# Flamingo block on one core: independent products between a group's last evacuation and its first dependent product, early octets loaded by ScalarE, finer waits

## The chip, the cores and the metric

One NeuronCore of a Trainium2 chip. The metric is the device time of one execution in microseconds, as the median of several runs. Engines in this text: TensorE (PE; PEld are its weight loads), VectorE (DVE), ScalarE (ACT), GpSimd (POOL), SyncE (SP; SPq and ACTq mark DMAs that SyncE and ScalarE issue). Sixteen DMA engines move the data.

## What is computed

A gated cross-attention block followed by a gated feed-forward block, 16 batches of 128 tokens of width 1024, all in float32. Cut to what matters:

```python
def attn(q, k, v):                       # 16 heads, dk = 16, 4 parts m per head
    qh, kh, vh = proj(q, Wq, bq), proj(k, Wk, bk), proj(v, Wv, bv)
    qh, kh, vh = (x + 0.1 * amp * einsum('bhsdi,hij->bhsdj', x, interference) for x in (qh, kh, vh))
    scores  = einsum('bhqdm,bhkdm->bhqkm', qh, kh) / sqrt(dk)
    weights = softmax(scores, axis=3)
    return einsum('bhqkm,bhkdm->bhqdm', weights, vh) @ Wo.T + bo

def ffn(x):
    base   = einsum('bsi,oi->bso', x, W_org)
    q      = einsum('bi,ki->bk', x.mean(axis=1), Wq)
    coeffs = softmax(einsum('bk,ek->be', q, lora_keys) / sqrt(K))
    h      = einsum('bsi,eir->bser', x, lora_down)
    return base + einsum('be,bser,ero->bso', coeffs, h, lora_up)

x = x + tanh(g_xattn) * attn(layernorm(x), ctx, ctx)
x = x + tanh(g_ffn)   * ffn(layernorm(x))
```

## The kernel before

Products of float32 precision are made from three float32r products: each operand is split into `hi` (ScalarE rounds, L149) and `lo` (VectorE subtracts, L152), and TensorE runs hi x hi, hi x lo, lo x hi (`three_products`, L159 to L161; 24 matmuls of 512 columns for a contraction over 1024).

The program has three phases with different schemes.

*Projections (0 to 614 us).* The order is a list of jobs (`Line`). A job is TensorE work into one of eight PSUM banks in turn, an optional ScalarE evacuation and a VectorE evacuation. Every engine goes through the list in order. TensorE waits for the bank (the job eight before must be emptied) and for `reads`, the number of the last job whose result it needs; since jobs are emptied in order, waiting for a number waits for everything before it. Steps for SyncE (loads and stores) stand in a `plan`, sorted by job number, and run in that order on its queue; each can wait. The batches are taken in four groups of four. A context tile is loaded and split into `place_a` or `place_b` (`ctx_jobs`). `k_job(g, c)` makes 128 output columns (chunk c) of the keys of group g, `q_job` the same of the queries, `v_job(b, half)` half of the values of batch b; keys and queries leave by `stage_hi` and `stage_lo` (L514, L512), two buffers in turn, each stored by six DMAs (L523). `mixed_chunk` multiplies a raw weight chunk by the head mixing matrix (L292) and splits the result. It is done for Wk and Wv in the first group, for Wq beside the values of the last group, where the inputs x are also normalised (`x_norm`, VectorE with a square root on ScalarE) and transposed (`x_jobs`, L326). During the last eight query products `wo_chunk` splits the output weights, DMAs from `v_out` lay rows of zeros and ones into the scratch tensors (L681, L682), four query tiles are cleared (L689, L695), and the first four octets are loaded (`load_early`, by SyncE, three DMAs each, L192 to L195).

*Attention (614 to about 1050 us).* 128 octets (8 heads of one batch) pass through an order written out by hand in slots: first pass of scores (L868), a maximum (L1008, L875, L1020), the maxima put into the query tile by a small DMA from `neg` (L803), second pass (L888), exponentials (L966), values (L903, each four octets), output projection (L851 to L853). Octet loads go by SyncE three slots ahead, once the octet six before has had its second pass.

*Feed-forward (to the end).* Job lists again. The LoRA products of the first group are begun before their coefficients are known: `h_job(0, 0, ..., "products")`, the scores (`first_scores`), `h_job(0, 1, ..., "products")`, then a VectorE-only job for the coefficients (`first_coefs`), two chunks of weights to split, and `spread_job`, which lays the coefficients along the rows (L1287 on TensorE, `coefc` by VectorE, L1290). The next product takes the bank that `spread_job` has eight jobs before it.

Of the kernel before, what the change touches and what calls it, by code (L numbers as in the profile page):

```python
# [15 lines left out]
class Job:  # L16

    def __init__(self, pe, dve, act=None, reads=0, pe_wait=None, act_wait=None, dve_wait=None,
                 act_pre=None, dve_pre=None, passed=None):
        self.pe, self.dve, self.act, self.reads = pe, dve, act, reads  # L20
        self.pe_wait, self.act_wait, self.dve_wait = pe_wait, act_wait, dve_wait
        self.act_pre, self.dve_pre, self.passed = act_pre, dve_pre, passed

class Line:
# [43 lines left out]
    def run_vector(self, dve):  # L68
        scaled = 0
        for n, job in enumerate(self.jobs):  # L70
            if job.dve_pre:
                job.dve_pre(dve)
            if job.act:
                scaled += 1
                dve.wait_ge(self.scaled, scaled)
            elif job.dve:
                self.wait_filled(dve, n + 1)
            if job.dve_wait:
                job.dve_wait(dve)
            if job.dve:  # L80
                job.dve(self.bank(n)).then_inc(self.emptied, 1)
            else:
                job.passed(dve).then_inc(self.emptied, 1)

def build(nc, x, ctx_cols, g_xattn, g_ffn, wq, wk, wv, biases, interference, amp, wo_rows, bo,
          w_org_rows, down_rows, lora_up, keys_cols, w_key, out):
    NB, S, D = x.shape
# [29 lines left out]
    with top:  # L117
# [303 lines left out]
        with proj, ExitStack() as st:  # L421
# [117 lines left out]
            def q_job(g, c):  # L539
                return projection_job(wq_end, t_end[NB + g * GB + GB - 1], 0, *x_place(g), bias_mixed[:, 1, c:c + 1],  # L540
                                      q_rows, c, g, 1)

            def v_job(b, half):
# [24 lines left out]
                job = Job(pe_fn, empty, reads=max(t_end[b], wv_end), dve_wait=stage_free)  # L568
# [34 lines left out]
            wk_end = {}  # L603
# [13 lines left out]
            for c in range(KC):  # L617
                job = k_job(0, c)
                if c == 0:

                    job.dve_pre = lambda dve: [link(dve.memset(v[:], 1.0)) for v in v_out]
                if c + 4 < KC:
                    wk_chunk(c + 4)
                wv_end = mixed_chunk(line, ring, wv, c, wv_hi, wv_lo)
            for g in range(NG):
                for b in range(g * GB, (g + 1) * GB):
                    v_job(b, 0)
# [6 lines left out]
                    for c in (2 * xb, 2 * xb + 1):  # L634
                        wq_end = mixed_chunk(line, ring, wq, c, w0_hi, w0_lo, reads=mix_scaled)
                    v_job(b, 1)
                    x_norm(xb, line.jobs[-4])
                    x_jobs(xb)
                if g + 1 < NG:
                    for c in range(KC):  # L640
                        job = k_job(g + 1, c)
                        if g + 2 == NG and c == 0:
                            def scale_mix(dve):

                                line.wait_filled(dve, wv_end)
                                link(dve.tensor_scalar(mix[:], mix[:], DK ** -0.5, None, ALU.mult))
# [6 lines left out]
            for g in range(NG):  # L653
                for c in range(KC):
# [42 lines left out]
                    if g == NG - 1 and KC - 1 - EARLY <= c < KC - 1:  # L697

                        def load_early(sp, o=c - (KC - 1 - EARLY)):
                            sp.wait_ge(s_cleared, EARLY)  # L700
                            sp.wait_ge(s_stage[o % 2], 96 * ((NG * KC + o) // 2 + 1))
                            load_kq(sp, o, (first_k, second_k, early_k[2], early_k[3])[o],
                                    early_q[o] if o else first_q, s_kq[o])
                        plan.append((len(line.jobs) + 0.7, load_early))
# [409 lines left out]
        with attend, ExitStack() as st:  # L1114
# [90 lines left out]
            def first_coefs():  # L1205
# [5 lines left out]
                return line.add(Job(None, coef_dve, dve_wait=lambda dve: dve.wait_ge(s_smalle, 1)))  # L1211
# [268 lines left out]
```

## Time and profile before

| | us |
|---|---|
| median of 3 runs | 1466.41 |
| lowest, highest | 1462.62, 1468.31 |
| profiled execution, its device time | 1468.58 |
| its span, first to last instruction | 1465.4 |
| TensorE busy in it | 1399.3 |
| VectorE, ScalarE, GpSimd busy | 674.2, 396.7, 234.8 |

All rows below come from the one profiled execution. A span leaves out some 3 us ahead of the first and behind the last instruction. TensorE's ends are modelled, and matmuls overlap: of 24 in a product each shows 0.39 us and starts some 0.23 us after the one before. A wait is given with the instruction that came last before it ended.

### The profile page before, as it was taken

The numbers are of one execution on the slowest core, as the hardware profiler recorded it, in microseconds if no ns is written. First come the engines' busy times: TensorE is split into PE (matmuls) and PEld (weight loads), VectorE is DVE, ScalarE is ACT, GpSimd is POOL, SyncE is SP. The second block draws the span as 40 slices with busy tenths as digits, with TensorE's granted clock in tenths as the row PEclk, the third lists the DMA queues.
The fourth block names the chain that finished last, engine by engine and source line by source line (L and its number), as shares of the span: only waits on it lengthen the run. The fifth ranks groups of instructions, "written<-read, shape, count | busy, mean of one in ns | idle before, by whom it ended". The sixth has DMA issues, their size and how long they took to land.

```text
span 1465.4 us, 22266 instructions
## 1 busy us (share of the span) xinstructions
PE 1399.3 (95%) x8592; PEld 1150.2 (78%) x8592; DVE 674.2 (46%) x1379; ACT 396.7 (27%) x736; POOL 234.8 (16%) x400
## 2 busy tenths in 40 slices
PE   7999999999999999878999999999979999999998
PEld 7887887878888888666777777877767878878787
DVE  5322131221555544456766666776766334244110
ACT  3311111111222222234545555454443110021100
POOL 0000000000000000014655555555600000000000
PEclk9999999999999999969999999999989999999999
DMA  6763645536547677966776776766542212202101
GB/s 201 205 170 130 142 145 137 151 124 143 178 152 186 161 188 183 259 198 201 216 229 193 232 222 205 222 200 199 179 179 87 86 44 75 83 17 85 43 30 57
DMA packets 181719, 224.86 MB, mean 153 GB/s; under 512 B 24048, under 2 KB 122352, under 8 KB 181616
## 3 DMA queue, kind: packets, MB, share of 16 engines
q1 hardware_dynamic: 166160, 189.11, 44.1%
q10 hardware_dynamic: 15456, 34.35, 7.3%
q8 instruction: 68, 1.11, 0.3%
q14 instruction: 35, 0.29, 0.1%
HBM read 136.89 MB, written 85.46 MB: 152 GB/s over the span
## 4 chain that ended last, share of the span: by engine, by line
PE 82%; DMA 8%; DVE 3%; SPq 3%; issue 2%; ACT 1%; POOL 0%; POOLq 0%; ACTq 0%; DVEq 0%
PE bank L159 19%; PE bank L161 19%; PE bank L160 19%; PE bank L903 4%; PE bank L868 4%; PE bank L888 3%; PE bank L292 3%; DMA q_in<-q_rows 3%; DMA early_q<-q_rows 3%; PE bank L851 2%; PE bank L853 2%; PE bank L852 2%; DMA first_q<-q_rows 2%; PE bank L326 2%; PE bank L875 1%
## 5 line engine op out<-in xcount | busy, mean ns | idle before, releaser
L1008 DVE TRANSPOSE_TENSOR_REDUCE part<-bank 128x16 f32<-128x512 f32 x256 | 167.8, 693 | 31.3 <-PE bank L868 29.4
L966 ACT ACTIVATE probT<-bank 128x512 f32<-128x512 f32 x256 | 138.6, 595 | 118.2 <-PE bank L888 118.1
L159 PE MATMUL bank<-place_a,w_hi 128*128 128x512 f32 x384 | 152.9, 398 | 7.9 <-DVE place_a L152 7.9
L512 DVE SCALAR_TENSOR_TENSOR stage_lo<-bank,bias_mixed,stage_hi 128x512 fp32r<-128x512 f32 x64 | 47.9, 749 | 232.6 <-ACT stage_hi L514 232.6
L161 PE MATMUL bank<-place_a,w_lo 128*128 128x512 f32 x384 | 151.1, 393 | 0.0
L160 PE MATMUL bank<-place_a,w_hi 128*128 128x512 f32 x384 | 150.9, 393 | 0.0
L514 ACT ACTIVATE stage_hi<-bank,bias_mixed 128x512 fp32r<-128x512 f32 x64 | 44.0, 688 | 265.0 <-PE bank L161 249.7
L851 PE MATMUL bank<-place_a,oT_hi 128*128 128x512 f32 x256 | 108.5, 424 | 0.5 <-POOL oT_lo L1095 0.4
L1351 DVE SCALAR_TENSOR_TENSOR raw_d<-bank,gates,raw_d 128x512 f32<-128x512 f32 x32 | 24.0, 750 | 173.2 <-PE bank L161 173.2
L159 PE MATMUL bank<-place_a,yT_hi 128*128 128x512 f32 x256 | 102.5, 400 | 0.0
L159 PE MATMUL bank<-place_b,place_a 128*128 128x512 f32 x256 | 100.5, 392 | 1.4 <-DVE place_c L152 1.4
L161 PE MATMUL bank<-place_a,yT_lo 128*128 128x512 f32 x256 | 101.2, 395 | 0.0
L160 PE MATMUL bank<-place_c,yT_hi 128*128 128x512 f32 x256 | 101.2, 395 | 0.0
L853 PE MATMUL bank<-place_a,oT_lo 128*128 128x512 f32 x256 | 101.0, 395 | 0.0
L852 PE MATMUL bank<-place_c,oT_hi 128*128 128x512 f32 x256 | 100.8, 394 | 0.0
L161 PE MATMUL bank<-place_b,place_a 128*128 128x512 f32 x256 | 99.8, 390 | 0.0
L160 PE MATMUL bank<-place_c,place_a 128*128 128x512 f32 x256 | 99.7, 390 | 0.0
L1059 POOL MEMSET q_in<- 98x1024 f32 x2 | 1.8, 951 | 610.2 <-PE bank L161 610.2
L159 PEld LDWEIGHTS bank<-place_a,w_hi 128*128 128x128 f32 x384 | 72.9, 190 | 24.2 <-DVE place_a L152 9.6
L560 DVE TENSOR_TENSOR v_out<-bank,bv_row 128x256 f32<-128x256 f32 x64 | 36.1, 605 | 115.0 <-PE bank L161 115.0
L161 PEld LDWEIGHTS bank<-place_a,w_lo 128*128 128x128 f32 x384 | 72.8, 190 | 15.5
L1020 DVE TENSOR_REDUCE negmax<-bank 32x32 f32<-32x128 f32 x128 | 35.7, 279 | 106.5 <-PE bank L875 106.5
(191 smaller groups left out, 2735.1 us busy)
## 6 DMA issues: line engine op xcount, KB each, us to landing
k_rows<-stage_hi SPq DMA_DIRECT2D x128, 128.0 KB, 2.4
v_pad<-v_out SPq DMA_DIRECT2D x32, 512.0 KB, 2.7
v_place<-v_pad ACTq DMA_DIRECT2D x32, 512.0 KB, 4.8
q_rows<-stage_hi SPq DMA_DIRECT2D x124, 128.0 KB, 2.4
early_q<-q_rows SPq DMA_DIRECT2D x128, 100.0 KB
q_in<-q_rows SPq DMA_DIRECT2D x84, 100.0 KB
early_k<-k_rows SPq DMA_DIRECT2D x42, 196.0 KB
k_in<-k_rows SPq DMA_DIRECT2D x42, 196.0 KB
```

Of the source, the lines that this page charges most:

```text
L159: nc.tensor.matmul(bank_ap, sh, mh, start=(i == 0), stop=False)
L160: nc.tensor.matmul(bank_ap, sh, ml, start=False, stop=False)
L161: last = nc.tensor.matmul(bank_ap, sl, mh, start=False, stop=(i == len(chunks) - 1))
L512: lambda bank: nc.vector.scalar_tensor_tensor(out=lo[:], in0=bank[:], scalar=bias, in1=hi[:].bitcast(F32), op0=ALU.add, op1=ALU.subtract),
L514: act=lambda bank: nc.scalar.activation(hi[:], bank[:], ACT.Identity, bias=bias),
L851: pe.matmul(o_bank[out][:], hi[:, c, :], wo_hi[:, k, cols], start=(k == 0), stop=False)
L852: pe.matmul(o_bank[out][:], hi[:, c, :], wo_lo[:, k, cols], start=False, stop=False)
L853: last = pe.matmul(o_bank[out][:], lo[:, c, :], wo_hi[:, k, cols], start=False, stop=(k == KC - 1))
L868: last = pe.matmul(dst, k_in[slot][:, p, :], q_in[slot][:, :, p, :], start=True, stop=True, skip_group_check=True)
L903: last = pe.matmul(v_bank[a][32 * p:32 * p + 32, i * P:(i + 1) * P], v_in[b % 2][:, 4 * (o % NOCT) + p, a, :], probT[o % NPT][:, p // 2, a ...
L966: act.activation(probT[o % NPT][:, i].rearrange("k a p q -> k (a p q)"), two_bank[i][:], ACT.Exp).then_inc(s_exp, 1)
L1008: dve.tensor_reduce(part[o % NS][:, :, 2 * i:2 * i + 2, :].rearrange("k a p b -> k a (p b)"), one_bank[i][:].rearrange("k (a b t) -> k a b ...
```

## The change

Five edits.

1. `v_job((g + 1) * GB, 0)`, the first half of the values of a group's first batch, stands before the eight key products of that group and no longer behind them.
2. In the last group the mixing of query chunks 6 and 7 stands behind the transposes of input tile 3, and the LayerNorm of that tile is attached to the first value job of the batch instead of a mixing job.
3. `wq_end` and `wv_end` are kept for each chunk: query product c waits for chunk c, and value halves for chunks 3 and 7.
4. `first_coefs` no longer waits for the TensorE jobs ahead of it in the list, only for the exponentials (`alone`).
5. `load_early` is issued by ScalarE ahead of its evacuation of query chunks 4 to 7 (octets 0 to 3). It was issued by SyncE behind the stores of chunks 3 to 6.

```diff
-            elif job.dve:
+            elif job.dve and not job.alone:
                 self.wait_filled(dve, n + 1)
...
             def q_job(g, c):
-                return projection_job(wq_end, t_end[NB + g * GB + GB - 1], 0, *x_place(g), bias_mixed[:, 1, c:c + 1],
+                return projection_job(wq_end[c], t_end[NB + g * GB + GB - 1], 0, *x_place(g), bias_mixed[:, 1, c:c + 1],
                                       q_rows, c, g, 1)
...
-                job = Job(pe_fn, empty, reads=max(t_end[b], wv_end), dve_wait=stage_free)
+                job = Job(pe_fn, empty, reads=max(t_end[b], wv_end[4 * half + 3]), dve_wait=stage_free)
...
             for g in range(NG):
+                def mix_query(chunks):
+                    for c in chunks:
+                        wq_end[c] = mixed_chunk(line, ring, wq, c, w0_hi, w0_lo, reads=mix_scaled)
+
                 for b in range(g * GB, (g + 1) * GB):
-                    v_job(b, 0)
+                    if b % GB or g == 0:
+                        v_job(b, 0)
                     if g + 1 < NG:
                         v_job(b, 1)
                         ctx_jobs(b + GB)
                         continue
 
                     xb = b - g * GB
-                    for c in (2 * xb, 2 * xb + 1):
-                        wq_end = mixed_chunk(line, ring, wq, c, w0_hi, w0_lo, reads=mix_scaled)
-                    v_job(b, 1)
-                    x_norm(xb, line.jobs[-4])
-                    x_jobs(xb)
+                    if xb + 1 < GB:
+                        mix_query((2 * xb, 2 * xb + 1))
+                        v_job(b, 1)
+                        x_norm(xb, line.jobs[-4])
+                        x_jobs(xb)
+                    else:
+                        x_norm(xb, line.jobs[-1])
+                        v_job(b, 1)
+                        x_jobs(xb)
+                        mix_query((2 * xb, 2 * xb + 1))
                 if g + 1 < NG:
+                    v_job((g + 1) * GB, 0)
                     for c in range(KC):
                         job = k_job(g + 1, c)
...
-                    if g == NG - 1 and KC - 1 - EARLY <= c < KC - 1:
-
-                        def load_early(sp, o=c - (KC - 1 - EARLY)):
-                            sp.wait_ge(s_cleared, EARLY)
-                            sp.wait_ge(s_stage[o % 2], 96 * ((NG * KC + o) // 2 + 1))
-                            load_kq(sp, o, (first_k, second_k, early_k[2], early_k[3])[o],
+                    if g == NG - 1 and KC - EARLY <= c:
+
+                        def load_early(act, o=c - (KC - EARLY)):
+                            act.wait_ge(s_cleared, EARLY)
+                            act.wait_ge(s_stage[o % 2], 96 * ((NG * KC + o) // 2 + 1))
+                            load_kq(act, o, (first_k, second_k, early_k[2], early_k[3])[o],
                                     early_q[o] if o else first_q, s_kq[o])
-                        plan.append((len(line.jobs) + 0.7, load_early))
+                        job.act_pre = load_early
...
-                return line.add(Job(None, coef_dve, dve_wait=lambda dve: dve.wait_ge(s_smalle, 1)))
+                return line.add(Job(None, coef_dve, dve_wait=lambda dve: dve.wait_ge(s_smalle, 1), alone=True))
```

In the changed kernel all line numbers from L20 on are one higher at first, and twelve higher from the attention phase on.

VectorE at the head of the second group, before: the last context tile (`place_a<-tin`) is followed by the evacuations of the eight key products (`stage_lo`), then come the values of batch 4 (`v_out`, two instructions for each half).

```order
L152 TENSOR_TENSOR place_a<-tin,place_a 128x512 [waits s_tin1,s_scaled_a] x2
L512 SCALAR_TENSOR_TENSOR stage_lo<-bank,bias_mixed,stage_hi 128x512 [waits s_scaled_a] x8
L560 TENSOR_TENSOR v_out<-bank,bv_row 128x16x16 [waits s_vst0,s_filled_a]
L560 TENSOR_TENSOR v_out<-bank,bv_row 128x16x16
L560 TENSOR_TENSOR v_out<-bank,bv_row 128x16x16 [waits s_vst1,s_filled_a]
```

VectorE at the same place, changed:

```order
L153 TENSOR_TENSOR place_a<-tin,place_a 128x512 [waits s_tin1,s_scaled_a] x2
L561 TENSOR_TENSOR v_out<-bank,bv_row 128x16x16 [waits s_vst0,s_filled_a]
L561 TENSOR_TENSOR v_out<-bank,bv_row 128x16x16
L513 SCALAR_TENSOR_TENSOR stage_lo<-bank,bias_mixed,stage_hi 128x512 [waits s_scaled_a] x8
L561 TENSOR_TENSOR v_out<-bank,bv_row 128x16x16 [waits s_vst1,s_filled_a]
```

The first half of the values of batch 4 has moved ahead of the eight keys; the heads of the third and fourth group change alike.

VectorE at the end of the last group, before: the LayerNorm of tile 3 ends (`tin`), three of the four evacuations of mixed weights follow (`w_lo`), then the second half of the last values, the transposed tile (`place_a<-bank`), and the LayerNorm of the next tile.

```order
L376 TENSOR_SCALAR tin<-tin,ln_mv_x,ln_rstd_x 128x1024 [waits s_chain]
L152 TENSOR_TENSOR w_lo<-bank,w_hi 128x4x128 [waits s_scaled_a] x3
L560 TENSOR_TENSOR v_out<-bank,bv_row 128x16x16 [waits s_vst1,s_filled_a]
L560 TENSOR_TENSOR v_out<-bank,bv_row 128x16x16
L152 TENSOR_TENSOR place_a<-bank,place_a 128x512 [waits s_scaled_a] x2
L364 BN_STATS ln_stats_x<-tin 128x6 [waits s_tin0,s_ln_done_x]
```

VectorE at the same place, changed:

```order
L377 TENSOR_SCALAR tin<-tin,ln_mv_x,ln_rstd_x 128x1024 [waits s_chain]
L561 TENSOR_TENSOR v_out<-bank,bv_row 128x16x16 [waits s_vst0,s_filled_a]
L561 TENSOR_TENSOR v_out<-bank,bv_row 128x16x16
L561 TENSOR_TENSOR v_out<-bank,bv_row 128x16x16 [waits s_vst1,s_filled_a]
L561 TENSOR_TENSOR v_out<-bank,bv_row 128x16x16
L153 TENSOR_TENSOR place_a<-bank,place_a 128x512 [waits s_scaled_a] x2
L153 TENSOR_TENSOR w_lo<-bank,w_hi 128x4x128 [waits s_scaled_a] x4
L365 BN_STATS ln_stats_x<-tin 128x6 [waits s_tin0,s_ln_done_x]
```

All four mixing jobs now stand behind the transposed tile, and the LayerNorm stands before both halves of the values.

SyncE at the end of the projections, before: stores of a query chunk (six DMAs, L523) with the load of an octet (three DMAs) between them.

```order
L523 DMA q_rows<-stage_hi 64x4x128 x2
L192 DMA first_k<-k_rows 98x512 [waits s_stage0,s_cleared]
L193 DMA first_q<-q_rows 50x512
L195 DMA first_q<-q_rows 50x512
L523 DMA q_rows<-stage_hi 64x4x128 [waits s_emptied_a]
L523 DMA q_rows<-stage_hi 64x4x128
L523 DMA q_rows<-stage_lo 64x4x128 x2
L523 DMA q_rows<-stage_hi 64x4x128 x2
L192 DMA second_k<-k_rows 98x512 [waits s_stage1,s_cleared]
```

ScalarE at the same stretch, changed: a split of output weights (`place_a<-raw`), a load, the evacuation of a query chunk.

```order
L150 ACTIVATE place_a<-raw 128x1024 [waits s_raw1,s_filled_a]
L193 DMA first_k<-k_rows 98x512 [waits s_stage0,s_cleared]
L194 DMA first_q<-q_rows 50x512
L196 DMA first_q<-q_rows 50x512
L515 ACTIVATE stage_hi<-bank,bias_mixed 128x512 [waits s_stage0,s_filled_a]
L150 ACTIVATE place_a<-raw 128x1024 [waits s_raw2,s_filled_a]
L193 DMA second_k<-k_rows 98x512 [waits s_stage1,s_cleared]
```

The four loads have left SyncE's queue, whose stores now follow one another, and stand on ScalarE, each one place further on in the list of query chunks.

## Rows read from the trace of the kernel before

**Rows 1.** The page's first part: busy us (share of the span) xinstructions.

```profile
PE 1399.3 (95%) x8592; PEld 1150.2 (78%) x8592; DVE 674.2 (46%) x1379; ACT 396.7 (27%) x736; POOL 234.8 (16%) x400
```

**Rows 2.** TensorE's waits, 0 to 614 us: total us, times, longest us.

```profile
PE bank L159 <- DVE place_a L152: 7.9, 5, 1.8
```

**Rows 3.** Timeline of TensorE: start us, us, operation, [idle before <- releaser].

```profile
92.34 0.50 PE L159 MATMUL bank<-place_b,place_a 128*128 128x512 f32 x1 [1.41 <-DVE place_c L152]
...
137.98 0.50 PE L159 MATMUL bank<-place_a,w_hi 128*128 128x512 f32 x1 [1.83 <-DVE place_a L152]
...
426.42 0.50 PE L159 MATMUL bank<-place_a,w_hi 128*128 128x512 f32 x1 [1.57 <-DVE place_a L152]
```

**Rows 4.** Timeline, 408 to 428 us, the last batch of the projections.

```profile
414.77 3.73 PE L292 MATMUL bank<-mix,raw 128*128 128x128 f32 x32
...
417.10 0.68 DVE L364 BATCH_NORM_STATS2 ln_stats_x<-tin 128x6 f32<-128x512 f32 x1
...
420.04 0.81 DVE L376 TENSOR_SCALAR tin<-tin,ln_mv_x,ln_rstd_x 128x1024 f32<-128x1024 f32 x1
```

**Rows 5.** Timeline, 1083 to 1094 us, the first coefficients of the feed-forward part.

```profile
1084.87 0.21 ACT L1259 ACTIVATE expo<-score 4x8 f32<-4x8 f32 x1 [9.74 <-DVE idle L1320]
...
1090.22 0.15 DVE L1208 RECIPROCAL ssum<-ssum 4x1 f32<-4x1 f32 x1 [5.38 <-PE bank L161]
...
1091.01 1.21 DVE L152 TENSOR_TENSOR place_c<-spare_hi,place_a 128x1024 fp32r<-128x1024 f32 x1
1091.13 1.05 PE L1287 MATMUL bank<-ident,coefw 4*128 4x4 f32 x8 [0.94 <-DVE coefw L1210]
...
1093.28 0.15 DVE L1290 COPY coefc<-bank 128x16 f32<-128x16 f32 x1
...
1093.49 0.50 PE L159 MATMUL bank<-yT_hi,place_b 128*128 128x512 f32 x1 [1.31 <-DVE coefc L1290]
```

**Rows 6.** Timelines of SyncE, ScalarE, VectorE and TensorE, 600 to 620 us.

```profile
600.61 0.58 SPq L192 DMA_DIRECT2D first_k<-k_rows  x1
...
601.95 1.24 SPq L523 DMA_DIRECT2D q_rows<-stage_hi  x2
...
616.67 1.25 SPq L192 DMA_DIRECT2D early_k<-k_rows  x1
...
619.12 0.64 SPq L803 DMA_DIRECT2D first_q<-neg  x1
...
604.23 0.69 ACT L514 ACTIVATE stage_hi<-bank,bias_mixed 128x512 fp32r<-128x512 f32 x1 [5.89 <-DMA q_rows<-stage_hi]
...
613.20 0.69 ACT L514 ACTIVATE stage_hi<-bank,bias_mixed 128x512 fp32r<-128x512 f32 x1 [3.66 <-DMA q_rows<-stage_hi]
...
614.59 1.30 DVE L1008 TRANSPOSE_TENSOR_REDUCE part<-bank 128x16 f32<-128x512 f32 x2
...
611.17 0.39 PE L161 MATMUL bank<-place_b,w_lo 128*128 128x512 f32 x1
```

**Rows 7.** Windows: us, busy time of engines (xinstructions), PEclk, DMA share, GB/s.

```profile
594.00:600.00 6.00, 6.00 (x28) 4.99 (x27) 3.20 (x3) 1.84 (x3) 0.00 (x0) 1.00 0.99 295
...
605.00:610.00 5.00, 5.00 (x23) 4.14 (x23) 3.11 (x4) 2.51 (x3) 0.00 (x0) 1.00 0.88 236
```

**Rows 8.** The page's DMA issues: count, KB each.

```profile
early_q<-q_rows SPq DMA_DIRECT2D x128, 100.0 KB
...
early_k<-k_rows SPq DMA_DIRECT2D x42, 196.0 KB
```

**Rows 9.** Timeline of TensorE in the first octets.

```profile
634.10 1.22 PE L888 MATMUL bank<-early_q,early_k 98*128 98x256 f32 x4 [0.89 <-DMA early_q<-neg]
...
637.07 1.23 PE L868 MATMUL bank<-early_q,second_k 98*128 98x256 f32 x4 [1.53 <-DMA early_q<-q_rows]
```

**Rows 10.** Windows in the first octets, columns as in rows 7.

```profile
620.00:625.00 5.00, 3.43 (x13) 2.60 (x13) 2.91 (x5) 0.05 (x1) 0.69 (x3) 0.50 0.79 247
...
640.00:680.00 40.00, 31.88 (x283) 25.24 (x276) 24.76 (x48) 16.55 (x30) 10.39 (x26) 0.78 0.65 194
```

More of the change, by code:

```diff
@@ L18, in __init__ @@
     def __init__(self, pe, dve, act=None, reads=0, pe_wait=None, act_wait=None, dve_wait=None,
-                 act_pre=None, dve_pre=None, passed=None):
+                 act_pre=None, dve_pre=None, passed=None,
+                 alone=False):
         self.pe, self.dve, self.act, self.reads = pe, dve, act, reads
         self.pe_wait, self.act_wait, self.dve_wait = pe_wait, act_wait, dve_wait
-        self.act_pre, self.dve_pre, self.passed = act_pre, dve_pre, passed
+        self.act_pre, self.dve_pre, self.passed, self.alone = act_pre, dve_pre, passed, alone
 class Line:
@@ L601, in bias_jobs @@
                         bv_row[:, half * HALF:(half + 1) * HALF], bank[:]), reads=end))
-            wk_end = {}
+            wk_end, wv_end, wq_end = {}, {}, {}
             def wk_chunk(c):
@@ L623, in build @@
                     wk_chunk(c + 4)
-                wv_end = mixed_chunk(line, ring, wv, c, wv_hi, wv_lo)
+                wv_end[c] = mixed_chunk(line, ring, wv, c, wv_hi, wv_lo)
             for g in range(NG):
+                def mix_query(chunks):
+                    for c in chunks:
+                        wq_end[c] = mixed_chunk(line, ring, wq, c, w0_hi, w0_lo, reads=mix_scaled)
                 for b in range(g * GB, (g + 1) * GB):
-                    v_job(b, 0)
+                    if b % GB or g == 0:
+                        v_job(b, 0)
                     if g + 1 < NG:
@@ L643, in scale_mix @@
                             def scale_mix(dve):
-                                line.wait_filled(dve, wv_end)
+                                line.wait_filled(dve, wv_end[KC - 1])
                                 link(dve.tensor_scalar(mix[:], mix[:], DK ** -0.5, None, ALU.mult))
```

## The prediction

> **What bounds the kernel now.** I read the page first: TensorE is busy 95% of the span [rows 1], so time can only come out of the moments in which TensorE stands still, or runs at half clock. The list of TensorE's waits up to the end of the projections (0 to 614 us) is short: apart from the start of the program it is 7.9 us on five waits for VectorE's `place_a` [rows 2] and one for `place_c`. The timeline of TensorE gives their places [rows 3]: 1.41 us before the product at 92.34 (the one for `place_c`), 1.83 us at 137.98 (the same stall, 1.82 us each, stands at 228.74 and at 317.90), and 1.57 us at 426.42. The fifth, 0.84 us at 25.40, is the very first product, which the change does not touch. In the feed-forward part TensorE waits 0.94 and 1.31 us around the first coefficients [rows 5]. Between lie the attention octets, whose start is bound otherwise: SyncE's queue, the DMA engines and a halved TensorE clock all meet there [rows 6, 7, 9, 10].
>
> **Part 1: an independent product at the head of each group (three places).** Before, the sequence at 137.98 is: value product (3, second half), evacuation of the last context tile of the next group, key product. The evacuation cannot begin before the value product is done, since it writes the place that product reads, and the key product waits for ScalarE and VectorE to do the first half tile [rows 3]. The change puts value product (4, first half) into this gap. It reads a tile evacuated three products earlier and weights long in place, and it lasts some 5.4 us (24 matmuls; a product of the same 24 in rows 5 is under way at 1084.87 and ends at 1090.19), three times the stall. So the stall goes whole, at all three group heads: 1.83 + 1.82 + 1.82 = 5.47 us. What the product leaves behind is a key product followed by value product (4, second half); neither waits for the other. Its VectorE evacuation and its store come before the eight key evacuations, in which both engines sit idle most of each 5.4 us. SyncE's queue gets the 512 KB store earlier and is else unchanged. Cost zero.
>
> **Part 2: the query weights of the last group (one place).** The first query product waits 1.57 us for the evacuation of the last transposes [rows 3]. The change moves four jobs of mixing (the row at 414.77, 3.73 us [rows 4]) from ahead of the last value product to behind these transposes. 3.73 us cover 1.57 us. The mixing needs only raw weights that were loaded a batch ago. In exchange the LayerNorm of the last input tile, 3.8 us of VectorE from 417.10 to 420.04 + 0.81 [rows 4], loses that cover, but it is moved ahead of both value products, 10.8 us, so it stays hidden with 7 us over. The evacuation of the first of the two is queued behind it on VectorE and nobody waits for that. The query product for output chunk 0 would still wait for chunk 7 of the mixing, and lose the gain again, were it not that each product now waits for its own chunk. Gain 1.57 us.
>
> **Part 3: finer wait for the value weights (one place).** The product at 92.34 waits 1.41 us for the evacuation of weight chunk 7 [rows 3]. It reads columns of chunks 0 to 3 alone, and the new wait says so. The next product, which needs chunk 7, comes 5.4 us later. Gain 1.41 us.
>
> **Part 4: the first coefficients.** The exponentials are ready on ScalarE at 1084.87 + 0.21 plus the read of the sum, but VectorE begins with the coefficients only at 1090.22, since its wait counts the product TensorE has under way [rows 5]. Behind it are queued two weight splits of 1.2 us each, then the copy of `coefc`, which TensorE waits for. Without this wait coefficients and splits are done by 1085.3 + 0.9 + 2 x 1.2 = 1088.6. TensorE goes from its product (ended at 1091.13 - 0.94 = 1090.19) straight to the spreading matmuls (1.05 us), VectorE copies `coefc` at once, and the next product follows 0.21 us after that copy starts, as it does now (1093.28 to 1093.49). That is 1090.19 + 1.05 + 0.04 + 0.21 = 1091.49 for 1093.49: gain 2.00 us. Its bounds are 1.3 (one of the two waits stays) and 2.25 (both go whole). The wait of 1.3 us for `up_lo` at 1113 hangs on a chain that starts with the product itself, so it moves along and stays.
>
> **Part 5: the first four octets loaded by ScalarE.** SyncE issues four loads between its stores; until its next issue they take 1.34, 1.36, 1.34 and 2.45 us, 6.5 us in all (the first from 600.61 to 601.95, the last from 616.67 to 619.12 [rows 6]; the two others are like the first). ScalarE's last evacuation waits for a store that such a load has held up: TensorE ends at 611.56, ScalarE starts at 613.20, and VectorE can take the first maximum only at 614.59 [rows 6]. With the loads gone from SyncE the store of chunk 4 goes 1.3 us earlier and that of chunk 5 1.5 us. The most it gives here is 613.20 - 611.56 = 1.6 us. Against it stands that the DMA engines are full: busy share 0.99 at 295 GB/s from 594 to 600, 0.88 from 605 to 610 [rows 7]. One load is 196 + 2 x 100 KB [rows 8], so 1.34 us of that rate, and the first load now goes ahead of the store of chunk 3, for whose landing ScalarE waits 5.89 us [rows 6]. If the bytes are what counts, one to two loads stand in front of a store that matters, a loss of 1.3 to 2.7 us. I take 1.0 us of the 1.6, because the share falls to 0.88 just where the last two stores go. ScalarE pays 1.2 us of issuing for each load, in stretches where it now idles 2 to 5.9 us; it waits there for nothing else, since the tiles that the loads fill are cleared ahead of chunks 1 and 2, and the first load comes ahead of chunk 4.
>
> Further on the earlier loads help twice: TensorE waits 0.89 us for a small transfer at 634.10 and 1.53 us for a load at 637.07 [rows 9]. That load is issued only when the second pass six octets earlier is over, so most of the 1.53 us is not the change's to give. I take 0.5 of 2.4 us. Part 5 together: 1.5 us, bounds -2.7 and +4.0.
>
> A rule of the Trainium skill speaks against more than this (DMA: Bandwidth & Descriptors, "Issuing engines are not separate DMA queues"): a second issuing engine saves only the sequencer's issue time, as all transfers share the same 16 engines. By that rule the part would be worth at most the 1.6 us of queue delay and nothing in bandwidth; the full DMA share of rows 7 is in line with it.
>
> **The sum.** 5.47 + 1.57 + 1.41 + 2.00 + 1.5 = 11.95, say 12.0 us. The profiled execution took 1468.6 us (its span 1465.4), so the same execution would take 1456.6; it stood 2.2 us above the median of 1466.4. Against the median the forecast is **1454.4 us**.
>
> **The rivals.**
> *The loads collide with the stores.* The bytes decide and part 5 costs 2.0 us in the middle of its lower bounds. For it: share 0.99. Against: the queue of SyncE, not the DMA, is full from 600 to 619. 1466.4 - 10.45 + 2.0 = 1458.0.
> *The edits to the products don't do what they say.* The moved product might find a wait of its own (its bank, which it takes from the job eight before) or the key product might wait as before. Then the 5.47 us stay: 1459.9. Against: eight jobs before is a product of batch 2, long evacuated.
> *The clock does not fall.* It stands at 0.50 of full speed from 620 to 625 [rows 10], and so up to 640, after TensorE had stood still from its first octet pass until VectorE's first maximum, begun at 614.59 [rows 6], was out. If the shorter pause keeps it up, the first pass of an octet, 1.23 us at half clock [rows 9], takes some 0.5 us less, for seven octets 3.5 us; the second passes and the first values product beside it may bring it to 5 us: 1449.4. Against: the first octets leave TensorE idle half of the time whatever the pause.
> *The clock stays down.* This one ends slower. From 640 to 680 the clock recovers only in part (mean 0.78) at 31.88 us of work [rows 10]. If the new spacing of loads and octets kept it at 0.50 there, that work would take 31.88 x 0.78 / 0.50 = 49.7 us, 17.9 us more: 1454.4 + 17.9 = 1472.3. It outweighs the gain from the point on at which two thirds of that stretch run at half clock. For it: the clock fell a second time there. Against: nothing in the change lengthens a pause. The Trainium skill says that the clock has two levels and falls after a pause (TensorE: Matmul & The Clock Gate, "What's actually happening"); the 0.50 of rows 10 agrees.
>
> **How the numbers follow.** Forecast 0.64, loads collide 0.14, products don't 0.08, clock stays up 0.09, clock stays down 0.05. The range takes in the bounds of part 5 on both sides, the clock that stays up, and some 2 us for the spread of medians: 1448.5 to 1460.0. About 0.5%, 7.3 us here, is what a measurement can tell from no change, so faster means below 1459.1. Forecast, colliding loads and the good clock lie there: 0.87, of which I take off 0.03 for spread. The product rival and most of the bad clock lie within: 0.13. Slower by over 0.5% needs more than 1473.7, past my price for the bad clock: 0.03.
>
> **What would show it.** In the changed profile TensorE's waits up to 614 us should hold nothing but the first product's 0.84 us and the start; five stalls at group heads gone. Mixing should stand between the last input transposes and the first query product. VectorE's coefficients should start near 1085 minus the shift, and the two waits around them shrink to one of 0.3 us. ScalarE's last evacuation should follow TensorE's last projection product within 1 us, and the queue of SyncE be free by some 613 minus the shift. The prediction is wrong if the stretch from the first octet to the last (614 to 1044, 430 us) changes by more than 3 us: no part of the sum lies inside it but the 0.5 us.

## The result

The changed kernel took 1445.73 us (median of 4 runs, 1443.85 to 1446.64) against 1466.87 us before, a ratio of 0.9859 with a 95% interval of 0.9835 to 0.9882. By the ratio that is 20.7 us less (the medians differ by 21.1) where 12.0 were forecast, and below the range of 1448.5 to 1460.0. The direction was right and the size was not. Measured again in two other sessions the changed kernel came to 0.9894 (0.9872 to 0.9916) and 0.9877 (0.9851 to 0.9903), 15.5 and 18.1 us less.

The profiled execution took 1444.85 us, its span 1442.9 us, 22.5 us less than the span before. Busy time of the engines, beside [rows 1]:

```profile
PE 1393.4 (97%) x8592; PEld 1146.2 (79%) x8592; DVE 674.5 (47%) x1379; ACT 397.3 (28%) x736; POOL 235.7 (16%) x400
```

The same 8592 matmuls kept TensorE busy 5.9 us less. An edit that only fills idle time cannot do that: here is the first sign that some matmuls ran faster than before. TensorE's waits from 0 to 610 us, beside [rows 2] (total us, times, longest us; the first row is of attention already):

```profile
PE bank L887 <- DVE part L1020: 5.3, 2, 4.3
...
PE bank L160 <- DVE place_a L153: 0.8, 1, 0.8
```

Only the 0.8 us of the very first product is left of the waits for `place_a`, and none for `place_c`. The products of [rows 3] now follow without a wait, and the mixing stands where it was put (timeline of TensorE):

```profile
91.71 0.47 PE L160 MATMUL bank<-place_b,place_a 128*128 128x512 f32 x1
...
409.97 1.03 PE L327 MATMUL bank<-ident,tin 128*128 128x128 f32 x8
410.84 3.74 PE L293 MATMUL bank<-mix,raw 128*128 128x128 f32 x32
414.33 0.48 PE L160 MATMUL bank<-place_a,w_hi 128*128 128x512 f32 x1
```

At the first coefficients, beside [rows 5]:

```profile
1065.93 0.21 ACT L1271 ACTIVATE expo<-score 4x8 f32<-4x8 f32 x1 [9.68 <-DVE idle L1332]
...
1066.27 0.15 DVE L1220 RECIPROCAL ssum<-ssum 4x1 f32<-4x1 f32 x1 [0.36 <-ACT expo L1271]
...
1071.18 1.05 PE L1299 MATMUL bank<-ident,coefw 4*128 4x4 f32 x8
...
1072.50 0.50 PE L160 MATMUL bank<-yT_hi,place_b 128*128 128x512 f32 x1 [0.27 <-DVE coefc L1302]
```

VectorE starts on the coefficients 0.1 us after the exponentials have ended, no longer 5 us, and one wait of 0.27 us is left of 0.94 and 1.31.

Where the 22.5 us of the two profiles lie, by marks that both traces have:

| stretch | before | after | gain | forecast |
|---|---|---|---|---|
| start to the last evacuation ahead of any edit (`stage_hi` of key chunk 7, first group) | 89.18 | 90.21 | -1.03 | 0 |
| from there to the first pass of octet 0 | 522.21 | 509.02 | 13.19 | 8.45 |
| first pass to the first `negmax` | 4.88 | 5.39 | -0.51 | 1.0 |
| first `negmax` to the 128th | 420.05 | 413.08 | 6.97 | 0.5 |
| from there to the scores (L1254) | 47.52 | 47.21 | 0.31 | 0 |
| scores to the product behind the coefficients | 9.65 | 7.59 | 2.06 | 2.00 |
| from there to the first product with `up_hi` | 19.93 | 18.39 | 1.54 | 0 |
| from there to the end | 351.98 | 352.01 | -0.03 | 0 |

The coefficients came to within 0.06 us of the sum. Three places gave something that no term of the sum held: the projections 4.7 us, the stretch behind the coefficients 1.5 us, the attention stretch 6.5 us. One gave less: the start of attention. The first row lies ahead of every edit and was 1.0 us longer after; in the 14 traces of this study it runs from 88.7 to 90.2 us.

### The profile page after: what moved, and what is told of

Same layout as the page of the kernel before. It is cut to its first block, busy times and chain, and to the rows that moved or that the text cites. A ratio compares the mean times of both kernels' runs of the same rounds, so it can differ in the third digit from the quotient of the medians.

```text
span 1442.9 us, 22265 instructions
## 1 busy us (share of the span) xinstructions
PE 1393.4 (97%) x8592; PEld 1146.2 (79%) x8592; DVE 674.5 (47%) x1379; ACT 397.3 (28%) x736; POOL 235.7 (16%) x400
## 4 chain that ended last, share of the span: by engine, by line
PE 82%; DMA 9%; DVE 2%; SPq 2%; issue 2%; ACT 1%; POOL 1%; POOLq 0%; ACTq 0%; DVEq 0%
PE bank L160 19%; PE bank L162 19%; PE bank L161 19%; PE bank L915 4%; DMA early_q<-q_rows 4%; PE bank L880 4%; PE bank L293 3%; PE bank L900 3%; PE bank L863 2%; PE bank L865 2%; PE bank L864 2%; DMA q_in<-q_rows 2%; PE bank L327 2%; DMA first_q<-q_rows 2%; PE bank L887 1%
## 5 line engine op out<-in xcount | busy, mean ns | idle before, releaser
L160 PE MATMUL bank<-place_a,w_hi 128*128 128x512 f32 x384 | 151.0, 393 | 0.8 <-DVE place_a L153 0.8
L161 PE MATMUL bank<-place_a,w_hi 128*128 128x512 f32 x384 | 149.4, 389 | 0.0
L162 PEld LDWEIGHTS bank<-place_a,w_lo 128*128 128x128 f32 x384 | 72.1, 188 | 15.2
```

Source lines behind the costliest of these rows:

```text
L160: nc.tensor.matmul(bank_ap, sh, mh, start=(i == 0), stop=False)
L161: nc.tensor.matmul(bank_ap, sh, ml, start=False, stop=False)
L162: last = nc.tensor.matmul(bank_ap, sl, mh, start=False, stop=(i == len(chunks) - 1))
```

## A second look at the trace of before

Behind the wait at 137.98 of [rows 3] the matmuls of the kernel before are not spaced as elsewhere. After the coefficients the same (timeline of TensorE before):

```profile
1093.83 0.39 PE L160 MATMUL bank<-yT_lo,place_b 128*128 128x512 f32 x1
1094.05 0.46 PE L161 MATMUL bank<-yT_hi,place_b 128*128 128x512 f32 x1
1094.31 0.63 PE L159 MATMUL bank<-yT_hi,place_b 128*128 128x512 f32 x1
1094.74 0.63 PE L160 MATMUL bank<-yT_lo,place_b 128*128 128x512 f32 x1
1095.16 0.63 PE L161 MATMUL bank<-yT_hi,place_b 128*128 128x512 f32 x1
```

Starts lie 0.23 us apart at first and 0.43 us from 1094.31 on. Windows around the first group head, before and then after (columns as in rows 7):

```profile
135.00:150.00 15.00, 13.17 (x52) 10.39 (x51) 3.08 (x5) 1.84 (x3) 0.00 (x0) 0.89 0.31 96
```

```profile
135.00:150.00 15.00, 15.00 (x68) 12.43 (x67) 4.20 (x7) 1.85 (x3) 0.00 (x0) 1.00 0.33 117
```

The granted clock is 0.89 on the mean there before, and 1.00 after. In before some eight matmuls run at 0.43 us spacing behind the first head, none behind the second, eight behind the third. So **theory A**: a stall of TensorE costs its idle time, a restart (what the first matmuls behind it lose against an unbroken row), and, where the clock falls behind it, 8 x 0.2 = 1.6 us more. **Theory B**: it costs its idle time alone, and the rest came from elsewhere. For the attention stretch **theory C**: the early loads on ScalarE bought it; **theory D**: it varies by itself from execution to execution.

## The experiments

### The new order at the three group heads alone

```diff
                 for b in range(g * GB, (g + 1) * GB):
-                    v_job(b, 0)
+                    if b % GB or g == 0:
+                        v_job(b, 0)
...
                 if g + 1 < NG:
+                    v_job((g + 1) * GB, 0)
                     for c in range(KC):
```

> The kernel before with the new product order at the three group heads alone. Theory A (a stall of TensorE costs its idle time and, where the clock falls behind it, a stretch of matmuls at half speed as well): no wait of some 1.8 us and no stretch of 0.43 us spacing behind the three group heads; 5.9 us of idle and restart plus 1.5 to 1.7 us for each head at which the clock fell (two of three in the trace of before), 7.5 to 10 us in all. Theory B (a stall costs its idle time alone, and the 3.2 us that the projections gained beyond the sum come from elsewhere): 5.5 us. The rest of the trace as in before.

Measured: 0.9929 of before (0.9901 to 0.9957), 10.4 us less by the ratio; the medians, 1459.92 and 1467.93, differ by 8.0 us. The trace settles the size better. No matmul at 0.43 us spacing at any head. From the start of the value product behind the wait of 1.41 us (92.34 before, 92.62 here) to the first pass of octet 0 it took 509.45 us, before 519.05 us: 9.60 us for three heads, where theory B has 5.5; the interval of the ratio, 6 to 15 us, leaves theory B out as well. Its feed-forward part is as before (9.64 and 19.88 us where the table has 9.65 and 19.93).

### The wait of the first coefficients alone

```diff
-            elif job.dve:
+            elif job.dve and not job.alone:
                 self.wait_filled(dve, n + 1)
```

> The kernel before, with the wait of the first coefficients alone taken away. Theory A: 2.0 us between the product ahead of the coefficients and the one behind, and 1.5 us more because the matmuls behind them no longer run at half clock (0.63 us each in before): 3.5 us. Theory B: 2.0 us. In the trace the distance from the scores (L1266) to the product behind the coefficients and on to the up_lo wait tells the two shares.

Measured: 0.9976 (0.9956 to 0.9995), 3.5 us less. Scores to product 7.59 us (9.65), product to `up_hi` 18.40 us (19.93): 2.06 and 1.53 us, the same two shares as in the profile after. This run keeps the stalls at the heads: the clock fell behind the first and not behind the second and third.

### Filler matmuls in the stalls at the heads

```diff
             if job.pe:
+                if job.warm:
+                    if n + 1 > ring:
+                        pe.wait_ge(self.emptied, n + 1 - ring)
+                    job.warm(self.bank(n))
                 if need:
...
                         job = k_job(g + 1, c)
+                        if c == 0:
+                            def warm(bank):
+                                for _ in range(8):
+                                    nc.tensor.matmul(bank[:], w0_hi[:, 0, 0:P], w0_hi[:, 0, 0:HALF], start=True, stop=True)
+                            job.warm = warm
```

> The kernel before, in which TensorE runs 8 extra matmuls of 512 columns into the free bank ahead of its wait at each of the three group heads (their result is overwritten). The stall becomes work of the same length, 8 x 0.227 = 1.8 us; the evacuation that ends the wait is where it was. Theory A (the clock falls because TensorE stands still): no matmul at 0.43 us spacing behind the first head in the trace, and 1.6 us less in the projections than before, 3.2 us where before drops twice. Theory B (the stall costs its idle time alone): no gain, and half-speed matmuls where they were.

The stretch around the first head in this run, the timeline of TensorE and then the window (columns as in rows 7):

```profile
136.23 1.97 PE L650 MATMUL bank<-w_hi 128*128 128x512 f32 x8
138.22 0.50 PE L164 MATMUL bank<-place_a,w_hi 128*128 128x512 f32 x1
138.57 0.40 PE L165 MATMUL bank<-place_a,w_hi 128*128 128x512 f32 x1
138.81 0.40 PE L166 MATMUL bank<-place_a,w_lo 128*128 128x512 f32 x1
139.04 0.40 PE L164 MATMUL bank<-place_a,w_hi 128*128 128x512 f32 x1
139.27 0.40 PE L165 MATMUL bank<-place_a,w_hi 128*128 128x512 f32 x1
```

```profile
135.00:150.00 15.00, 14.98 (x67) 12.04 (x66) 3.09 (x5) 2.37 (x4) 0.00 (x0) 1.00 0.39 113
```

The key product starts where it did, 2.2 us behind the start of the value product's last matmul, but the matmuls behind it keep their 0.23 us from the second on: nothing but the standstill was taken away, and the clock stayed at 1.00. It stayed so at all three heads. From the value product at 92.58 to octet 0 this run took 515.89 us: 3.16 us less than before with two falls, 1.6 us less than the runs with one fall (517.41 with the coefficients' wait alone taken away, 517.51 with the loads alone moved), and 6.44 us more than with the new order. So one fall costs 1.6 us, and a stall of 1.82 us costs 6.44 / 3 = 2.15 us without a fall. The rows have 0.28 of the 0.33 us of restart: a matmul shows 0.39 us (its end is modelled) where the next one starts after 0.23, and ahead of a wait nothing overlaps its last 0.16 us; and the second matmul starts 0.35 us behind the first (138.22, 138.57), 0.12 more than usual.

As a whole the run does not show its gain: 1.0010 of before (0.9994 to 1.0027), 1466.55 us. Its first seven octets took 26.9 us (25.1 to 25.9 in the traces with neither moved loads nor filler), the way to them 5.8 us (3.3 to 4.9 there), and one group of eight octets 29.8 us. The expected 1.6 us is smaller than what the attention stretch adds or takes, and the total decides nothing here. Why the first octets were slow in this run, and in the next one (28.8 us for seven), was not looked into.

### Half of the filler

The same with 4 matmuls.

> The kernel before with 4 extra matmuls (0.9 us) ahead of the wait at each of the three group heads, so that half of each stall is left. Theory A: the shorter the standstill, the rarer the fall: no half-speed matmuls behind the first head, where the three traces without filler or new order all show them. If they are there all the same, a standstill of 0.9 us is enough.

In the profile at all three heads a wait of 0.92 us is left and no matmul at 0.43 us spacing follows.

```profile
136.27 1.07 PE L650 MATMUL bank<-w_hi 128*128 128x512 f32 x4
138.26 0.50 PE L164 MATMUL bank<-place_a,w_hi 128*128 128x512 f32 x1 [0.92 <-DVE place_a L157]
```

From 92.61 to octet 0 it took 515.84 us, the same as with full filler. It was executed once, so its total says nothing. Over all traces of this study the clock fell behind 4 of 9 stalls of 1.82 us at a head (three of three at the first, once at the third), at none of 3 stalls of 0.92 us, at none of the six of 1.57 us ahead of the first query product and none of the six of 1.41 us at 92 us. Behind the two close waits at the coefficients, 0.94 and 1.31 us, it fell in all five traces that have them. That is a count, not a rule: three traces have the full stall at all three heads, two have filler there.

### The early loads back on SyncE

```diff
-                        job.act_pre = load_early
+                        plan.append((len(line.jobs) + 0.7, load_early))
```

with the condition and the waits of before.

> The changed kernel with the four early loads back on SyncE behind the stores of chunks 3 to 6. Theory C (the loads on ScalarE bought the 7.0 us by which the attention stretch is shorter in the profile after): 5 to 7 us slower than the changed kernel, attention stretch near 420 us. Theory D (the loads collide with the stores at the start, 0.5 us lost there, and the attention stretch varies by itself): within 1.5 us of the changed kernel, some 1445, last evacuation of the projections within 1.7 us of TensorE's last product as in before.

Measured: 0.9894 (0.9866 to 0.9921), attention stretch 420.31 us. This looked like theory C, but the changed kernel had been measured in another session. So both ran once more on one chip:

> The changed kernel with the four early loads back on SyncE, again, beside the changed kernel. Theory C: 1449 to 1453. Theory D: within 2 us of the changed kernel.

> The changed kernel once more, on one chip with its version that leaves the early loads on SyncE. Theory C (part 5 shortens the attention stretch): 413 to 415 us from the first to the last maximum in the profile, and 4 to 7 us faster than the version without part 5. Theory D (that stretch varies by itself from run to run): 413 to 424 us, and within 2 us of the version without part 5.

Measured: loads on SyncE 0.9897 (0.9879 to 0.9916), 1449.47 us; changed kernel 0.9894 (0.9872 to 0.9916), 1448.30 us. No difference; and the changed kernel's attention stretch was 423.2 us this time, longer than the 420.0 us with the loads on SyncE. Theory D stands.

### The early loads alone

The kernel before with edit 5 of the change and nothing else.

> The kernel before with the four early loads moved to ScalarE alone. Theory C: 5 to 7 us faster than before. Theory D: within 1.5 us of before, with the last evacuation 0.4 us later against TensorE's last product. The three group heads are untouched here, so the trace also shows how often the clock falls behind a stall of 1.8 us: theory A expects it at some of them again and not at others.

Measured: 0.9992 (0.9976 to 1.0008), no difference to be told. The clock fell behind the first head, not behind the others. ScalarE's last evacuation starts 2.9 us after TensorE's last product has ended, 1.2 us later than before.

All traces with and without the moved loads, without those that have filler:

| | loads on ScalarE (4 traces) | loads on SyncE (5 traces) |
|---|---|---|
| first pass to first maximum (`negmax`) | 5.39, 5.01, 6.20, 6.22 | 4.88, 4.42, 4.48, 3.89, 3.26 |
| TensorE's last product to ScalarE's last evacuation | 2.0, 1.7, 2.9, 2.9 | 1.6, 1.1, 1.1, 0.7, 0.0 |
| first to eighth | 24.1, 23.9, 24.2, 24.6 | 25.1, 25.6, 25.4, 25.9, 25.3 |
| first to 128th | 413.1, 423.2, 418.3, 421.5 | 420.1, 423.2, 424.3, 420.3, 420.0 |

(In both columns the order is: the changed kernel or the kernel before first, then the runs. On ScalarE: after, after again, after third, loads alone. On SyncE: before, new order alone, coefficients alone, and twice the changed kernel with its loads on SyncE.) On the way to the first maximum the moved loads cost 1.5 us on the mean, nearly all of it ahead of the last evacuation, and over the next seven octets they give 1.2 us back. In the first three rows the two columns do not overlap. Timelines of ScalarE, before and then after, show the cost:

```profile
596.70 0.69 ACT L514 ACTIVATE stage_hi<-bank,bias_mixed 128x512 fp32r<-128x512 f32 x1 [2.50 <-DMA q_rows<-stage_hi]
```

```profile
586.08 0.69 ACT L515 ACTIVATE stage_hi<-bank,bias_mixed 128x512 fp32r<-128x512 f32 x1 [4.18 <-DMA q_rows<-stage_hi]
...
593.53 0.69 ACT L515 ACTIVATE stage_hi<-bank,bias_mixed 128x512 fp32r<-128x512 f32 x1 [5.82 <-DMA q_rows<-stage_hi]
...
601.44 0.69 ACT L515 ACTIVATE stage_hi<-bank,bias_mixed 128x512 fp32r<-128x512 f32 x1 [3.94 <-DMA q_rows<-stage_hi]
```

The evacuation at 586.08 stood at 596.70 before; less the shift of 12.16 us, that is 1.5 us later. It waits for the store of chunk 2, in the midst of which the first load was now issued. The one behind it, waiting for the store of chunk 3, is 1.5 us later too (593.53 for 604.23 [rows 6]). The last, at 601.44, starts 2.05 us after TensorE's last product has ended; before it was 1.64 us [rows 6]. It waits for the store of chunk 5. SyncE began to issue that store at 595.03; before, at 607.32, less the shift 595.16. So it went out 0.1 us earlier only, since the evacuation of chunk 5 was itself 1.5 us late, and the evacuation that waits for it came 0.4 us later.

### What makes the attention stretch long

The changed kernel a third time:

> The changed kernel a third time, as the other side of the two runs with filler matmuls and as one more sample of the attention stretch (413.1 and 423.2 us so far). Theory D (the stretch varies from execution to execution with octet loads that come late): between 413 and 424 us, and where it is long, one group of eight octets takes 28 us or more instead of 26, with a TensorE clock below 1.00 in it.

Measured: 0.9877 (0.9851 to 0.9903), stretch 418.3 us, and in it one group of eight octets of 29.3 us where 26 are usual, with a clock of 0.94 and 0.89 there. The run with the new order alone has such a group of 29.2 us. Timeline of TensorE in it, and then the window around it (columns as in rows 7):

```profile
895.06 0.74 PE L870 MATMUL bank<-early_q,early_k 98*128 98x256 f32 x4 [2.43 <-DMA early_q<-q_rows]
...
896.41 0.63 PE L853 MATMUL bank<-place_a,oT_hi 128*128 128x512 f32 x1
896.84 0.63 PE L854 MATMUL bank<-place_c,oT_hi 128*128 128x512 f32 x1
```

```profile
890.00:900.00 10.00, 7.57 (x34) 6.06 (x33) 4.30 (x10) 3.76 (x7) 3.28 (x7) 0.83 0.53 143
```

TensorE waits 2.43 us for an octet load and the clock falls behind it: the same two costs as at a group head, but at a place that changes from one execution to the next. Of the 14 traces, nine have one group of eight octets of some 28 us or more (28.0 to 29.8) behind the first sixteen, and in six of the nine the clock falls once in it. The profiles of before and after have no such group, so a single late load does not explain the 7 us between these two. What does, and why loads are late in one execution and not in another, stays open.

### Filler in the first octets

Here TensorE stands still between short matmuls and the clock is at 0.50 [rows 10]. Can filler keep it up, as at the heads?

```diff
+                def warm(s):
+                    if s == 0:
+                        pe.wait_ge(project_line.emptied, project_line.last_use(turn[4]))
+                    for _ in range(12 if s == 0 else 2):
+                        pe.matmul(v_bank[0][:], wo_hi[:, 0, 0:P], wo_hi[:, 0, 0:HALF], start=True, stop=True,
+                                  skip_group_check=True)
+
...
                     first_pass(s, 1)
+                    if s < FIRST_V:
+                        warm(s)
```

> The changed kernel with extra matmuls on TensorE in the first seven slots of the attention part (12 of 512 columns in slot 0, 2 in each of the next six, into a bank that the values product overwrites later), placed where TensorE waits for VectorE's maximum. Theory A (standing still is what halves the clock, so work without use keeps it up): PEclk 1.00 in place of 0.50 from the first octet to the seventh, 3.5 to 5 us less from the first maximum to the eighth (24 us in the profile after, some 20 here). Theory B (the clock is not what bounds these octets, VectorE's chain is, or the filler itself delays the chain): PEclk may rise, the stretch stays at 24 us or gets longer.

> The same filler matmuls, with the four early loads back on SyncE. If the filler works, the first seven octets run faster and want their loads earlier: theory C2 (the loads on ScalarE are worth more once the octets run at full clock): 1 to 3 us slower than the version with the filler and the loads on ScalarE. Theory D: equal within 1.5 us.

> The changed kernel with the early loads on SyncE and twice the filler in the first octets: 16 matmuls in slot 0, 4 in each of the next six. With 2 for each slot the clock held up to 605 or 611 us and then fell. Theory A: with 4 TensorE hardly stands still, the clock stays at 1.00 up to the values product, and the first seven octets take 20 to 21 us in place of 25.3: 1442 to 1446. Theory B: the clock falls all the same; then 4 fillers at half speed (1.7 us) stand in the chain and each octet takes 0.5 us more, 28 to 29 us for seven, 1448 to 1452.

The second is the first with the four loads issued as before, the third is the second with 16 and 4 matmuls in place of 12 and 2. Measured: 0.9890 (0.9859 to 0.9921) with the loads on ScalarE, 0.9855 (0.9825 to 0.9885) with the loads on SyncE, and 0.9886 (0.9867 to 0.9905) with twice the filler and the loads on SyncE. First to eighth maximum 24.7, 25.3 and 24.7 us, where theory A had some 20. With 2 matmuls in each slot the clock did not hold: it fell at 606 us in the first run and at 610 us in the second. With 4 it did what theory A says, and still next to nothing was gained. Windows of the run with twice the filler:

```profile
605.00:610.00 5.00, 3.42 (x18) 2.40 (x17) 2.76 (x6) 0.00 (x0) 0.89 (x4) 1.00 0.88 261
610.00:615.00 5.00, 3.41 (x21) 2.52 (x20) 2.30 (x5) 3.23 (x5) 0.55 (x3) 1.00 0.78 223
615.00:620.00 5.00, 3.81 (x21) 2.87 (x21) 2.91 (x5) 1.31 (x3) 0.78 (x4) 1.00 0.91 266
```

The clock is 1.00 up to 620 us. TensorE's waits in the same run, 598 to 660 us, tell where part of the time went:

```profile
PE bank L880 <- DMA early_q<-q_rows: 5.9, 4, 3.1
...
PE bank L880 <- DMA q_in<-q_rows: 1.6, 2, 0.9
```

In the same window the profile after has 4.0 and 1.5 us for these, and the two runs with the loads on SyncE and no filler have 3.9 and 2.7, and 5.0 and 1.0 us. So TensorE waits 0.9 to 2.0 us longer for loads: at full clock the octets are ready for their keys and queries sooner, and the loads, at DMA shares of 0.8 to 0.9, are not there. Against the traces with the loads at the same place (25.1 to 25.9 us) the run with twice the filler is 0.4 to 1.2 us faster over these seven octets, in one trace. That the loads took the rest of the expected 4 to 5 us is not shown: the filler itself may have held up the second passes. The difference between moving the loads and not moving them, expected at 1 to 3 us, went the other way (1450.19 us on ScalarE, 1446.89 us on SyncE), with intervals that overlap. None of the three can be told from the changed kernel (0.9877 in the session of the first two), so no version here is shown to beat it.

## Why the prediction was wrong

**Where it failed: the price of a stall.** The mechanism of the products was right, all five stalls went; the term was too small. Part 1 of the sum took "the stall goes whole: 1.83 + 1.82 + 1.82 = 5.47 us", idle time alone. It measured 9.60 us against the trace of before (new order alone), in three terms: 5.47 us of idle, 0.97 us of restart (a stall of 1.82 us costs 2.15), and 3.16 us for the two falls of the clock. The last was in the prediction's reach: it read the clock of the first octets and of 640 to 680 us, and made rivals of it there, but did not look at the clock behind the stalls that it priced. At the six heads of the two filler runs data and evacuations were as before and no fall came, against four at nine full stalls, and in no trace did it fall at a head without a stall: the fall goes with the standstill.

**Part 2 and part 3** were forecast at 1.57 + 1.41. From the table, 13.19 less 9.60 leaves 3.6 us for the two. The marks part them: from `stage_hi` to the value product 3.16 us before and 1.50 after, 1.7 us for part 3, and so 1.9 us for part 2. The clock did not fall behind these stalls; the surplus of 0.6 us is what two restarts of 0.33 us would give. Neither was run alone.

**Part 4**, the mechanism and its 2.00 us were right (2.06). The 1.5 us behind it are the same omission: both waits there are short, and the clock fell all the same.

**Part 5** was forecast at 1.5 us, 1.0 at the start and 0.5 further on, and the moved loads cannot be told from nothing (0.9992, and 0.9894 against 0.9897). The step "the store of chunk 4 goes 1.3 us earlier and that of chunk 5 1.5 us" failed: the first load goes out in the midst of the store of chunk 2, into DMA engines that are full, the stores land later and hold up ScalarE, the store of chunk 5 goes out 0.1 us earlier only, and the first maximum comes 1.5 us later against the products, on the mean of the traces. That was the rival of colliding loads, and at this place it was right. The gain lies further on, 1.2 us over the first seven octets where 0.5 was forecast. The rule of the Trainium skill (DMA: Bandwidth & Descriptors, "Issuing engines are not separate DMA queues") holds here: 6.5 us of SyncE's issue time were freed, and no time was gained that the runs can tell.

**The attention stretch** differs by 7.0 us between the two profiles, and that was no effect of an edit that any run could show: with the changed kernel it was 413.1, 423.2 and 418.3 us, with versions that leave the loads alone 420.0 to 424.3 us. The prediction had called itself wrong if this stretch changed by more than 3 us. That sign came true, but a single pair of profiles can't carry it: the stretch differs by 10 us between profiles of one kernel. The range had 2 us for the spread of medians and named no such source. The other sign that failed is the last evacuation, 2.05 us after TensorE's last product where it was to be within 1 us.

Put right, the sum is 9.60 + 3.6 + 2.06 + 1.54 and nothing for part 5, 16.8 us, or 15.2 us where the clock falls only behind the first head, as in two further traces with these stalls. The two later sessions gave 15.5 and 18.1 us. The first gave 20.7 us, of which some 4 us remain beyond this sum. So the miss of 8.7 us is made up of 6.3 us by which the stalls were priced too low, 1.5 us that part 5 did not give, which goes the other way, and the 4 us left. With 16.8 us the median would have been 1450, still inside the range. That it came out below took the 4 us that stay open; its profile has the shortest attention stretch of all. Whether its chip or its hour made the stretch short in all four runs stays open.

**The rivals.** The edits to the products do what they say. The clock of the first octets stayed at 0.50, so the rival in which it stays up did not happen. Its price of 5 us looks too high as well: where filler kept the clock up to 620 us, at most 1.2 us came of it. The clock that stays down did not happen: from 628 to 668 us, which is 640 to 680 less the shift, it was 0.79 on the mean, before 0.78.

## What to carry to other kernels

Price a stall of TensorE with the granted clock and the spacing of the matmuls behind it, not with its idle time alone: here 1.8 us of idle cost 2.15 us, and 3.7 us where the clock fell. Where independent work exists, putting it into the stall takes all three costs away; matmuls without use take away only the fall, and where the loads come late as well, little of that shows. A transfer issued earlier on another queue still goes through the same DMA engines; look at what lands behind it.

## What the runs showed of the hardware that was not expected

A standstill of 1.82 us at full load was enough for the granted clock to go to its lower level (1.2 of 2.4 GHz; matmuls of 512 columns 0.43 us apart in place of 0.23) for some eight matmuls, at 4 of 9 such places, and two waits of 0.94 and 1.31 us with 1 us of small matmuls between them did it in five of five. The Trainium skill (TensorE: Matmul & The Clock Gate, "Why this matters for your kernels") advises against idle gaps between bursts of matmuls and names longer ones than these there; in these traces shorter ones were enough. A single pause of 0.92 us (3), 1.41 us (6) or 1.57 us (6) never did it.
